# A ramp with one batch's rows: first pair on its own path, second batch's rows moved into steps 4 to 8

## The reference

```
h   = layernorm(x)
q   = h @ Wq;  k = concat(h @ Wk1, ctx @ Wk2);  v = concat(h @ Wv1, ctx @ Wv2)   # 8 heads of 64, 768 keys
x   = x + tanh(g_xattn) * (softmax(q k^T / 8) v @ Wo + bo)
y   = layernorm(x)
moe = sum over the top 2 of 8 experts e: w_e * (gelu(y @ w1[e] + b1[e]) @ w2[e] + b2[e])
x   = x + tanh(g_ffn) * (moe + gelu(y @ ws1 + bs1) @ ws2 + bs2)
```

## Time and profile before

| | |
|---|---|
| runs, us | 152.44, 153.16, 153.36 (median 153.16) |
| profiled execution, us | 152.52, its span 150.6 |
| mean granted TensorE clock | 0.998 |
| busy us: PE, DVE, ACT, POOL | 142.1, 102.6, 114.5, 115.6 |
| exponentials of steps 0, 1, 5 start at, us | 18.87, 22.96, 35.11 |
| loads in the ramp, us from issue to landing | x 2.7, Wk2 and Wk1 4.2, Wq 4.4 |

### The profile page before, as it was taken

The page is one execution under the profiler, slowest core; times in us unless marked ns, Lnnn a source line. Parts: engine busy times, 40 slices in busy tenths (PEclk is TensorE's granted clock), DMA queues, the critical chain, the costliest instruction groups (busy, mean ns, idle before and its releaser), DMA issues.

```text
span 150.6 us, 4483 instructions
## 1 busy us (share of the span) xinstructions
PE 142.1 (94%) x1844; PEld 109.5 (73%) x1844; DVE 102.6 (68%) x216; ACT 114.5 (76%) x192; POOL 115.6 (77%) x101
## 2 busy tenths in 40 slices
PE   7899879979999999999999998999999999999992
PEld 5533544447666665666788797999999998999991
DVE  1588898987868688676875355535768885865631
ACT  3445789999798888979639999855679898768720
POOL 6508989769969999898968898997356589885830
PEclk9999999999999999999999999999999999999999
DMA  5789995000000000000000000040000001000001
GB/s 140 222 294 294 328 333 159 0 0 7 4 2 4 2 0 4 0 4 0 4 0 4 0 4 4 0 139 4 0 0 4 4 0 39 0 0 4 0 0 35
DMA packets 10253, 7.71 MB, mean 51 GB/s; under 512 B 1101, under 2 KB 8442, under 8 KB 10234
## 3 DMA queue, kind: packets, MB, share of 16 engines
q1 hardware_dynamic: 10234, 7.44, 16.6%
HBM read 7.18 MB, written 0.26 MB: 49 GB/s over the span
## 4 chain that ended last, share of the span: by engine, by line
PE 71%; ACT 11%; DVE 9%; issue 4%; DMA 2%; SPq 0%; DVEq 0%; ACTq 0%
PE banks L1003 13%; PE banks L1004 11%; PE banks L1005 11%; PE banks L1286 8%; ACT prob L656 5%; PE banks L1182 4%; DVE part L833 3%; PE banks L1184 3%; PE banks L1132 3%; PE banks L1183 3%; ACT p_hi L664 3%; ACT v_hi L645 3%; PE banks L1202 3%; PE banks L1100 2%; DMA wf<-in_ctx_dram 2%
## 5 line engine op out<-in xcount | busy, mean ns | idle before, releaser
L556 POOL TENSOR_TENSOR p_lo<-prob,p_hi 128x1024 f16<-128x1024 f32 x23 | 49.0, 2134 | 7.2 <-ACT p_hi L664 6.8
L722 ACT ACTIVATE prob<-banks,b1T 128x256 f32<-128x256 f32 x72 | 28.1, 474 | 10.1 <-PE banks L1005 10.1
L656 ACT ACTIVATE prob<-banks 128x1024 f32<-128x1024 f32 x24 | 24.5, 1021 | 8.1 <-PE banks L1150 8.1
L833 DVE TENSOR_REDUCE part<-banks 128x2 f32<-128x1024 f32 (+1 forms) x24 | 29.0, 1214 | 0.1
L579 POOL TENSOR_TENSOR k_both<-prob,k_both 128x1024 f16<-128x1024 f32 x11 | 23.4, 2132 | 6.6 <-ACT k_both L730 5.9
L664 ACT ACTIVATE p_hi<-prob 128x1024 f16<-128x1024 f32 x24 | 25.4, 1056 | 0.7
L1182 PEld LDWEIGHTS banks<-v_hi,p_hi 128*128 128x128 f16 x192 | 17.4, 98 | 3.4 <-issue 2.3
L1003 PE MATMUL banks<-x2h,wf 128*128 128x256 f16 x72 | 19.6, 273 | 0.0
L1005 PE MATMUL banks<-x2h,wf 128*128 128x256 f16 x72 | 19.6, 273 | 0.0
L1004 PE MATMUL banks<-x2h,wf 128*128 128x256 f16 x72 | 19.6, 272 | 0.0
L1182 PE MATMUL banks<-v_hi,p_hi 128*128 128x65 f16 x192 | 19.2, 195 | 0.4 <-DVE o_sb L861 0.4
(11 more groups left out here) (153 smaller groups left out, 346.1 us busy)
## 6 DMA issues: line engine op xcount, KB each, us to landing
ring<-in_L_ffn_w_dram SPq DMA_DIRECT2D x16, 256.0 KB, 4.9
wf<-in_ctx_dram SPq DMA_DIRECT2D x2, 256.0 KB, 5.3
ring<-in_L_xattn_Wk_dram SPq DMA_DIRECT2D x2, 256.0 KB, 4.2
ring<-in_L_xattn_Wv_dram SPq DMA_DIRECT2D x2, 256.0 KB, 5.9
ring<-in_L_ffn_ws_dram SPq DMA_DIRECT2D x2, 256.0 KB, 5.8
x_sb<-in_x_dram SPq DMA_DIRECT2D x1, 256.0 KB, 2.7
ring<-in_L_xattn_Wq_dram SPq DMA_DIRECT2D x1, 256.0 KB, 4.4
wo<-in_L_xattn_Wo_dram SPq DMA_DIRECT2D x1, 256.0 KB, 6.7
```

The costliest lines, as they stand in the source:

```text
L556: nc.gpsimd.tensor_tensor(p_lo[:, u % RINGP, :, :].rearrange("p a n -> p (a n)"), prob[:, u % RINGE, :], p_hi[:, u % RINGP, :, :].rearrang ...
L656: nc.scalar.activation(prob[:, u % RINGE, :], units(u).rearrange("p a n -> p (a n)"), ACT.Exp, scale=DH ** -0.5 / S_SCORE).then_inc(exp_do ...
L722: nc.scalar.activation(hid[:, k % NHID, c * T1:(c + 1) * T1], span(2 * (k % 2), HC * T1)[:, c * T1:(c + 1) * T1], ACT.Gelu, bias=b1T[:, e ...
L833: nc.vector.tensor_reduce(dst, src, AX_X, ALU.max).then_inc(part_done, 1)
```

## The change

x is loaded in two halves, the second behind Wv2. The ramp's `tx` item holds batch 0 alone (256 columns); `tx` of batch 1 is an item of step 6. The queries become `q0` items (batch 0, one pair, 256 columns) and `q1` items (batch 1, two pairs in one bank), the latter in steps 7 and 8.

The first pair's keys and queries are no items any more. Keys go to bank 4 and 5, queries to bank 7 (they were in bank 6). ScalarE copies the keys' `hi` and then the raw keys into the third buffer of `prob`; VectorE copies the queries' `hi`; ScalarE then copies the raw queries; POOL computes both `lo` from the raw copies. Keys of pair 1 wait for the raw copy, since they use the same banks.

The splits of Wk2, Wk1 and Wq stand behind `tc` and `tx` on both engines. `scores` is cut into `open_scores` (the three products) and `close_scores` (the shift); for unit 0 the opening part stands in step -2, ahead of the shift row. Statistics of batch 1 come at the end of VectorE's step 4, their power in POOL's step 5 behind `p_lo` of unit 4, their normalisation at the end of VectorE's step 5. The bias is added to batch 1's rows into `acc`. On POOL all three parts of the shared expert's split move to steps 1, 3 and 4. The counts of warm-up matmuls change (9, 4, 12 become 4, 8, 3, 8).

```diff
-PRE = [(("tc", 0), 0), (("tx", 0), 2), (("k", 0, 0), 4), (("q", 0), 6)]
+PRE = [(("tc", 0), 0), (("tx", 0), 2)]
+K0_BANK, Q0_BANK = 4, 7
...
-    6: [(("v", 1, 0), 5)],
-    7: [(("k", 1, 0), 4)],
+    6: [(("tx", 1), 4), (("v", 1, 0), 5)],
+    7: [(("k", 1, 0), 4), (("q1", 0), 7)],
+    8: [(("q1", 2), 7)],
...
-WARM_START, WARM_LAYERNORM, WARM_MAX, WARM_STEP = 14, 9, 4, 12
+WARM_START, WARM_LAYERNORM, WARM_KEYS, WARM_MAX, WARM_STEP = 14, 4, 8, 3, 8
+STATS1_STEP, POW1_STEP, NORM1_STEP, BIAS1_STEP = 4, 5, 5, 7
...
-SPLIT_BEFORE = {1: [WK2, WK1], 2: [WQ]}
-SPLIT_BY_ACT = {1: [WK2, WK1, WQ]}
+RAMP_SPLITS = [WK2, WK1, WQ]
...
+        raw0 = prob[:, RINGE - 1, :]
+        k0_out = span(K0_BANK, KEYS)
+        q0_out = banks[:, Q0_BANK, 0:T1]
+        k0_rows = [k_nat[:, hl, 0, 0, :] for hl in range(2)]
+        q0_rows = [q_nat[:, hl, 0, 0, :] for hl in range(2)]
...
-            sp.dma_start(x_sb[:, :, :], x_d).then_inc(ld_x, 16)
+            sp.dma_start(x_sb[:, 0:QT, :], x_d[:, 0:QT, :]).then_inc(ld_x, 16)
...
             load_a(WV2)
-
-
+            sp.dma_start(x_sb[:, QT:, :], x_d[:, QT:, :]).then_inc(ld_x1, 16)
+
+
+            load_a(WV1)
             load_f(0)
-            for w in (WV1, WO):
-                load_a(w)
+            load_a(WO)
...
-            nc.gpsimd.tensor_tensor(rstd[:, 0:NT], vare[:, 0:NT], c_mhalf[:, 0:NT], ALU.pow).then_inc(rstd_ready, 1)
+            nc.gpsimd.tensor_tensor(rstd[:, 0:QT], vare[:, 0:QT], c_mhalf[:, 0:QT], ALU.pow).then_inc(rstd_ready, 1)
...
-            early_hi(0)
...
+            pool.wait_ge(k0_hi, 1)
+            pool.wait_ge(k0_raw, 1)
+            nc.gpsimd.tensor_tensor(k0_rows[1], raw0[:, 0:KEYS], k0_rows[0], ALU.subtract).then_inc(k0_lo, 1)
+            pool.wait_ge(q0_hi, 1)
+            pool.wait_ge(q0_raw, 1)
+            nc.gpsimd.tensor_tensor(q0_rows[1], raw0[:, KEYS:KEYS + T1], q0_rows[0], ALU.subtract).then_inc(q0_lo, 1)
+            lo_by_pool(WV2)
             add_bias()
-            lo_by_pool(WV2)
-            early_scaled(0)
             lo_by_pool(WV1)
...
+                if i == POW1_STEP:
+                    pool.wait_ge(var_ready, 2)
+                    nc.gpsimd.tensor_tensor(rstd[:, QT:NT], vare[:, QT:NT], c_mhalf[:, QT:NT],
+                                            ALU.pow).then_inc(rstd_ready, 1)
                 if i == 1:
+                    early_hi(0)
+                if i == 3:
+                    early_scaled(0)
+                if i == 4:
                     early_lo(0)
...
             for n in range(len(PRE)):
                 item_of(n)
+            for w in RAMP_SPLITS:
+                split_a(w)
+            act.wait_ge(k0_ps, 1)
+            nc.scalar.activation(k0_rows[0], k0_out, ACT.Copy, scale=1.0 / S_W).then_inc(k0_hi, 1)
+            nc.scalar.activation(raw0[:, 0:KEYS], k0_out, ACT.Copy, scale=1.0 / S_W).then_inc(k0_raw, 1)
+            act.wait_ge(q0_ps, 1)
+            act.wait_ge(q0_hi, 1)
+            nc.scalar.activation(raw0[:, KEYS:KEYS + T1], q0_out, ACT.Copy, scale=1.0 / S_W).then_inc(q0_raw, 1)
             tanh_gates()
...
-            row_statistics(x_sb, 0, NT)
-            for n in range(len(PRE) - 1):
+            row_statistics(x_sb, 0, QT)
+            normalise_rows(x_sb, 0, QT, 1)
+            for n in range(len(PRE)):
                 item_of(n)
+            for w in RAMP_SPLITS:
+                split_a(w)
+            dve.wait_ge(q0_ps, 1)
+            nc.vector.tensor_scalar(q0_rows[0], q0_out, 1.0 / S_W, None, ALU.mult).then_inc(q0_hi, 1)
...
-                    if (p, c) == (0, UPP - 1):
-                        item_of(len(PRE) - 1)
+                if i == STATS1_STEP:
+                    dve.wait_ge(ld_x1, 16)
+                    row_statistics(x_sb[:, QT:, :], QT, QT)
+                if i == NORM1_STEP:
+                    normalise_rows(x_sb[:, QT:, :], QT, QT, 2)
...
+                elif kind == "q1":
+                    pe.wait_ge(item_lo, ITEMS.index(("tx", 1)) + 1)
+                    for m in range(2):
+                        p = item[1] + m
+                        last = three(dst[:, m * T1:(m + 1) * T1], w_pair(WQ, slice(p * P, (p + 1) * P)),
+                                     x_pair(slice(T1, 2 * T1)))
...
-            keep_warm(WARM_MAX, 2)
+            keep_warm(WARM_KEYS, 6)
+            keys_of(k0_out, 0, 0).then_inc(k0_ps, 1)
+            wait_split(pe, WQ)
+            three(q0_out, w_pair(WQ, slice(0, P)), x_pair(slice(0, T1))).then_inc(q0_ps, 1)
+            keep_warm(WARM_MAX, 6)
...
             for i in range(CHUNK0, STEPS):
+                if 0 < i < NU:
+                    open_scores(i)
                 if 0 <= i < NU:
-                    scores(i)
+                    close_scores(i)
...
                 if i == -2:
-                    pe.wait_ge(part_done, 2)
-                    keep_warm(WARM_STEP, 2)
+                    keep_warm(WARM_STEP, 6)
+                    open_scores(0)
```

More of the change, by code:

```diff
@@ L403, in item_out @@
             kind = ITEMS[n][0]
-            return span(BANK[n], KEYS) if kind == "k" else banks[:, BANK[n], :]
+            if kind == "k":
+                return span(BANK[n], KEYS)
+            return banks[:, BANK[n], 0:T1] if kind in ("tx", "q0") else banks[:, BANK[n], :]
+        raw0 = prob[:, RINGE - 1, :]
[3 more added lines that the diff above has]
+        q0_rows = [q_nat[:, hl, 0, 0, :] for hl in range(2)]
         block = stack.enter_context(nc.Block())
@@ L768, in row_statistics @@
                     last = nc.vector.bn_aggr(mv[:, first + t, :], stats[:, first + t, :])
-                    if first > 0 and t == tiles - 1:
+                    if first >= NT and t == tiles - 1:
                         last.then_inc(var_ready, 1)
@@ L773, in row_statistics @@
                 settle()
-                if first > 0:
+                if first >= NT:
                     return
@@ L1028, in read_out, with keys_of @@
                     pe.wait_ge(item_lo, n)
+            def keys_of(dst, b, p):
+                pair = slice(p * P, (p + 1) * P)
+                wait_split(pe, WK2)
+                pe.wait_ge(item_lo, ITEMS.index(("tc", b)) + 1)
+                three(dst[:, 0:T2], w_pair(WK2, pair), c_pair(slice(b * T2, (b + 1) * T2)))
+                wait_split(pe, WK1)
+                pe.wait_ge(item_lo, ITEMS.index(("tx", b)) + 1)
+                return three(dst[:, T2:KEYS], w_pair(WK1, pair), x_pair(slice(b * T1, (b + 1) * T1)))
             def item_of(n):
@@ L1035, in item_of @@
                 if kind == "tx":
[L1036 to L1039 removed]
+                    b = item[1]
+                    if b == 0:
+                        keep_warm(WARM_LAYERNORM, 6)
+                    for t in range(QT):
+                        pe.wait_ge(xn_ready, QT * b + t + 1)
+                        last = nc.tensor.transpose(dst[:, t * P:(t + 1) * P], xn[:, QT * b + t, :], ident[:, :])
                 elif kind == "tc":
@@ L1115, in shift_row, with score_tiles, open_scores @@
                 nc.tensor.transpose(shift_ps_rows, nmax[:, p % 2, :], ident[:, :]).then_inc(shift_ps, 1)
-            def scores(u):
+            def score_tiles(u):
+                p, third = divmod(u, UPP)
+                return [(n, half, slice(n * T1, (n + 1) * T1),
+                         slice((KT2 * third + n) * P, (KT2 * third + n + 1) * P))
+                        for n in range(KT2) for half in range(2)]
+            def open_scores(u):
                 p, third = divmod(u, UPP)
@@ L1147, in scores @@
                     pe.wait_ge(shift_done, p + 1)
-                for n, half, cols, keys in tiles:
+                for n, half, cols, keys in score_tiles(u):
                     rows = slice(DH * half, DH * half + DH)
```

98 lines of the change are left out of this document (55 added, 43 removed), and 6 rows, old and new, of the table LATE.

## The result

| | before | after |
|---|---|---|
| median of the runs, us | 152.8 (152.41 to 153.5, 6 runs) | 156.21 (155.52 to 156.6, 6 runs) |
| profiled execution, its span, granted clock | 152.52, 150.6, 0.998 | 155.52, 153.7, 0.993 |
| exponentials of steps 0, 1, 5 start at, us | 18.87, 22.96, 35.11 | 15.57, 19.54, 31.50 |
| exponentials of steps 6, 7, 8, 9 | 38.34, 41.60, 44.31, 46.69 | 35.88, 41.44, 44.81, 48.21 |

The ratio after to before is 1.0207, 95% interval 1.0167 to 1.0247: slower by 1.7 to 2.5%. The forecast was 153.0 with a range up to 154.7, and the time lies outside it.

What follows compares the result with a forecast made beforehand. TensorE and POOL, both full from step 5 on, and before 35 us a chain of waits across engines were taken to bound it. 2.1 us gained against 2.6 paid made 0.5 lost: 152.52 to 153.0, range 151.2 to 154.7.

Steps and rivals of the forecast that it cites:

- (a) to (d): Ramp to step 5: half load, parallel copies, queries' low half off the chain, narrower queries; 2.1 us ahead at step 5.
- (a): Start of the ramp: x loaded by half lets the context land 0.3 us earlier; keys start at 8.7 against 9.00.
- the clock rises sooner: Ramp: less idle time before the context's transposes, first keys at 0.22 and 0.11; 0.65 + 0.25 less, 152.1; chance 0.15.
- (e): Step 6: two added transposes on TensorE at the higher clock level cost 0.30 us.
- (f): Steps 7 and 8: the second batch's queries, 12 matmuls of 256 columns, cost 1.30 us on TensorE.
- (h): Between batch 1's first v and the next keys: one more low half on VectorE, 0.2 us; new statistics mostly hidden.
- (g): Step 5: VectorE's normalisation of the second half waits 1.1 us for POOL's late power, costing 0.8; bounds 0 to 1.1.
- the sign that the prediction had named for it: Sign of a right forecast: VectorE waits 0.8 to 1.4 us for POOL's power at the second half's normalisation.
- step 9 starts no earlier than before: Sign of a right forecast: step 9, behind the steps that pay, starts no earlier than in the kernel before.
- a late clock: Ramp: TensorE stands still more and its clock rises later; about 1.7 us, 154.7; chance 0.13.
- a ramp that is not shortened: Ramp: context lands no earlier, keys wait for the splits; gain 0.4 instead of 0.9, 153.5 or 153.9; chance 0.10.
- the dear ends of (a) and (g): Unfavourable bounds: the smaller load gains 0 in the ramp, POOL's late power costs 1.1 us; chance 0.02.

Runs made afterwards that it cites:

- e8_both: e6_norm_early with the shared expert's three parts on POOL put behind step 4; 153.3 us, ratio 1.0009 to the kernel before.
- e9_early_vector: e6_norm_early with the two normalised rows put back on VectorE in step 5, power still early; 153.82 us, ratio 1.0053 to the kernel before.
- f1_fill: The changed kernel plus ten unread matmuls of 256 columns between the two row transposes of step 6; 154.68 us, ratio 1.0143 to the kernel before.
- e6_norm_early: The changed kernel with batch 1's statistics and POOL's power one step earlier, the two rows on ScalarE; 151.51 us, ratio 0.9935 to the kernel before.
- e3_before_plus: The kernel before plus three unread VectorE instructions from SBUF to SBUF: one 128x2 in step 4, two 128x128 in step 5; 155.06 us, ratio 1.0148.
- e2_vare_pool: The changed kernel with the 128x2 variance plus epsilon moved from VectorE to POOL, rows left on VectorE; 156.44 us, ratio 1.0262 to the kernel before.
- e10_late_scalar: e6_norm_early with statistics and POOL's power back in steps 4 and 5, rows on ScalarE; two executions, 153.09 and 154.53 us, too few for an interval.
- e5_again: The changed kernel once more, unaltered, for a second profile; 156.04 us, ratio 1.0229 to the kernel before.
- e1_norm_scalar: The changed kernel with batch 1's normalisation moved from VectorE to POOL and ScalarE in step 5; 156.33 us, ratio 1.0248 to the kernel before.

## Why the prediction was wrong, point by point

**The ramp, (a) to (d): right in the sum, and the rival on the clock came on top.** In e8_both, whose ramp is that of the change, the clock rose late as in the kernel before:

```profile
4.88 1.09 PE L1109 MATMUL banks<-ident,wf 128*128 128x128 f32 x4 [0.67 <-DMA wf<-in_ctx_dram]
8.97 0.61 PE L1056 MATMUL banks<-cT,wa 128*128 128x512 f16 x1
9.37 0.63 PE L1057 MATMUL banks<-cT,wa 128*128 128x512 f16 x1
...
17.21 1.02 ACT L698 ACTIVATE prob<-banks 128x1024 f32<-128x1024 f32 x1 [0.29 <-PE banks L1239]
```

There the first exponential is at 17.21 (forecast 17.3) and that of step 5 at 33.16: 1.95 us ahead of 35.11, against 2.1 forecast. The 0.3 that (a) gave to the smaller load did not show there: the context's transposes start at 4.88, as before, and in the profiles with the change's ramp anywhere from 4.22 to 4.99. With the early rise of the kernel after the lead is 3.6. So the rival "the clock rises sooner" came true: 0.22 in the first keys, as its sign was named. Its price (0.9) depends on the place of the rise. The ramps of e9_early_vector and f1_fill are alike and their context's transposes start at 4.96 and 4.99; the first exponentials are at 17.31 and 15.88, 1.4 us apart, and in f1_fill the clock had risen ahead of these transposes (0.63 us for the four, 1.09 in e9_early_vector). In e6_norm_early and the kernel after the first exponential is 1.0 and 1.6 earlier than in e8_both, but the context's transposes too start 0.46 and 0.66 earlier. The rise scatters: of all 17 profiles here 13 have it before the first keys and 4 within them, the kernel before with idle additions (e3_before_plus) among the 13, its first exponential at 18.12. The Trainium skill, "TensorE: Matmul & The Clock Gate", part 1, which the prediction had cited, says that the place differs between runs of one kernel. These profiles agree in kind: the late rises and the early ones are of kernels with the same ramp, while the two profiles of the changed kernel rose alike (first keys 0.23 and 0.22 apart).

**(e), (f) and (h), added matmuls and one more low half: right in the sum.** 0.30 + 1.30 + 0.2 = 1.8 us. In e6_norm_early, where neither lock nor late power is left, the steps 5 to 9 are 13.36 us, 11.58 before: 1.78 more. Of the three terms only the queries were measured by themselves.

**(g), the late power: right as a mechanism, and not what was paid.** POOL's power ended at 35.70, before VectorE came (35.92), because the whole of POOL's chain was earlier and VectorE was late itself. The wait of 1.1 was not there; the sign that the prediction had named for it was missing. Where VectorE or ScalarE came in time it was: 1.34 (e2_vare_pool), 2.41 (e10_late_scalar). That step 9 starts no earlier than before, another sign that was named, came true for a different reason, which is luck.

**The step that failed: the durations of VectorE's moved instructions.** In (h) the statistics were to "lie mostly in the 0.57 that VectorE waits", in (g) the two rows were priced at 0.27 each "by the slope from 512 columns". Both took durations from rows in which POOL stood still or in which VectorE read PSUM, and moved the instructions to a place where POOL never stops. Measured: 1.44 instead of 0.17 for one, 2.94 instead of 0.54 for two. In the kernel before, with nothing else of the change, two such rows took 2.19 and the time rose by 1.5% (e3_before_plus). Exponentials, steps 5 to 9, kernel before (ScalarE):

```profile
38.34 1.02 ACT L656 ACTIVATE prob<-banks 128x1024 f32<-128x1024 f32 x1 [0.39 <-PE banks L1150]
41.60 1.02 ACT L656 ACTIVATE prob<-banks 128x1024 f32<-128x1024 f32 x1 [0.39 <-PE banks L1150]
44.31 1.02 ACT L656 ACTIVATE prob<-banks 128x1024 f32<-128x1024 f32 x1
46.69 1.02 ACT L656 ACTIVATE prob<-banks 128x1024 f32<-128x1024 f32 x1 [0.28 <-PE banks L1150]
```

With the table above, the distances of steps 5 to 9:

| us | 5 to 6 | 6 to 7 | 7 to 8 | 8 to 9 | 5 to 9 |
|---|---|---|---|---|---|
| before | 3.23 | 3.26 | 2.71 | 2.38 | 11.58 |
| after, first profile | 4.38 | 5.56 | 3.37 | 3.40 | 16.71 |
| after, second (e5_again) | 4.37 | 7.05 | 3.19 | 3.20 | 17.81 |
| e6_norm_early (neither cause) | 3.50 | 3.24 | 3.22 | 3.40 | 13.36 |
| e9_early_vector (rows locked) | 3.23 | 4.94 | 3.37 | 3.39 | 14.93 |
| e10_late_scalar (power late) | 5.97 | 2.73 | 3.72 | 3.40 | 15.82 |

Against the kernel before, the changed kernel loses 1.15 and 2.30 in steps 5 and 6 of its first profile, where its waits stand behind the lock (against e6_norm_early 0.88 and 2.32, the lock and the late power that it hides), 1.5 more to the clock in its second, part of which the next two steps give back (0.4), and 1.7 in steps 7 and 8, where the queries stand. 3.6 us of lead at step 5 (3.3 in the second profile) become 1.5 (2.9) of lag at step 9, which is 1.8 (3.2) at the last computation.

**The sign was in the trace of before.** VectorE's eleven casts of the expert stage from SBUF to SBUF, 128x512, take 0.41 to 0.51 us in six cases and 1.22 to 1.87 in five; the longest ends (128.27) 0.28 after POOL's pair of subtractions (127.99). VectorE, then POOL:

```profile
121.38 0.42 DVE L946 CAST k_both<-prob 128x512 f16<-128x512 f32 x1
126.40 1.87 DVE L946 CAST k_both<-prob 128x512 f16<-128x512 f32 x1 [1.09 <-ACT prob L722]
...
123.77 4.22 POOL L579 TENSOR_TENSOR k_both<-prob,k_both 128x1024 f16<-128x1024 f32 x2
```

**The end of the span.** The last store took 2.5 us to land in the first profile of after, 1.2 before. It does not go with the change: e5_again has 1.2, e3_before_plus 2.6.

**Range and chances.** The slow side was given 0.15 and up to 154.7, by a late clock, a ramp that is not shortened, or the dear ends of (a) and (g). No rival had a mechanism in steps 4 to 6 apart from POOL's power.

## What to carry to other kernels

Before a VectorE copy, cast or tensor-scalar instruction from SBUF to SBUF is moved, look at what POOL does at the new place, and price it at the time until POOL's running instruction ends, once for each instruction. Look for the same operation with two different durations in the trace. A duration from a quiet part of the kernel is a lower bound. If two causes stand one behind the other, a version that takes away one can win nothing by where it puts the work (e1_norm_scalar, e2_vare_pool): make the version without both first, then put each back.
